# A decoder layer on one core: token turns, row statistics and roots of the last stage put in another order and on other engines

## The reference

```python
x = _layernorm(x + self_attention(x))        # 32 heads of 16, 8 key heads, causal, rotary
x = _layernorm(x + cross_attention(x, ctx))  # 32 heads of 128, 8 key heads, mask, rotary
x = _layernorm(x + clustered_ffn(x))
```

```python
def _L0_ffn_ref(input, weight, bias, centroids, assignments):
    x = input.reshape(-1, shape[-1])
    dots = jax.nn.softmax(x @ centroids.T / TEMPERATURE, axis=-1)   # 64 clusters, 0.1
    hits = dots > THRESHOLD                                          # 0.01
    query_sel = jnp.any(hits, axis=1)          # per token
    cluster_sel = jnp.any(hits, axis=0)        # per cluster, over ALL tokens
    row_sel = cluster_sel[assignments]         # per output feature
    dense = x @ weight.T + bias
    return jnp.where(query_sel[:, None] & row_sel[None, :], dense, 0)

def _layernorm(x, axis=-1, eps=1e-05):
    m, v = jnp.mean(x, ...), jnp.var(x, ...)
    return (x - m) / jnp.sqrt(v + eps)
```

## Time and profile before

| | |
|---|---|
| median of 3 runs | 811.86 us (811.58 to 813.31) |
| profiled execution, its own time | 813.68 us |
| span of the profiled execution | 811.8 us |
| PE busy | 757.1 us, 93% of the span |
| DVE busy | 600.1 us, 74% |
| POOL busy | 401.7 us, 49% |
| ACT busy | 321.0 us, 40% |
| mean granted clock of TensorE | 0.989 |

### The profile page before, as it was taken

One profiled execution on the slowest core, in us unless ns is written; L12 is line 12 of the kernel. 1 busy time (PEld: TensorE's weight loads), 2 busy tenths in 40 slices (PEclk: granted clock), 3 DMA queues, 4 the chain that ended last, 5 costly groups with the idle time before them and its releaser, 6 DMA issues.

```text
span 811.8 us, 13867 instructions
## 1 busy us (share of the span) xinstructions
PE 757.1 (93%) x4800; PEld 648.5 (80%) x4800; DVE 600.1 (74%) x1150; ACT 321.0 (40%) x680; POOL 401.7 (49%) x383
## 2 busy tenths in 40 slices
PE   4789999989999999999999999999999999999985
PEld 3677777779878887888888888888888888888763
DVE  4678888877877686677768767766776866788766
ACT  3555555563334333342333334323323423334314
POOL 7566666674544544453454445354444544354104
PEclk9899999999999999999999999999999999999998
DMA  9600004012253232322223322223322223230002
GB/s 235 149 18 17 16 16 120 3 56 53 67 142 79 53 77 58 100 53 52 78 54 77 96 57 52 52 78 76 79 78 52 52 53 98 44 93 2 1 0 103
DMA packets 107873, 53.52 MB, mean 66 GB/s; under 512 B 80448, under 2 KB 96960, under 8 KB 107840
## 3 DMA queue, kind: packets, MB, share of 16 engines
q1 hardware_dynamic: 107008, 51.51, 25.1%
q10 hardware_dynamic: 576, 1.05, 0.4%
q0 software_dynamic: 256, 0.52, 0.2%
HBM read 32.62 MB, written 2.10 MB: 43 GB/s over the span
## 4 chain that ended last, share of the span: by engine, by line
PE 67%; DVE 17%; issue 6%; POOL 4%; ACT 2%; DMA 2%; SPq 2%; DVEq 0%; POOLq 0%; ACTq 0%
PE bank L730 17%; PE bank L665 17%; PE bank L491 10%; DVE arena_r L1571 4%; PE s_bank L744 4%; PE bank L541 2%; PE s_bank L746 2%; PE bank L565 2%; PE bank L714 2%; DVE small L1659 2%; PE bank L883 2%; DVE arena_f L1653 1%; PE s_bank L714 1%; DMA arena_f<-in_L_attn_Wo 1%; PE s_bank L565 1%
## 5 line engine op out<-in xcount | busy, mean ns | idle before, releaser
L992 ACT ACTIVATE arena_r<-bank 128x256 fp32r<-128x256 f32 (+2 forms) x249 | 105.2, 459 | 219.0 <-PE bank L697 85.4
L730 PE MATMUL bank<-arena_r 128*128 128x512 f32 x768 | 191.5, 398 | 0.0
L665 PE MATMUL bank<-arena_r 128*128 128x512 f32 x720 | 185.2, 400 | 2.6 <-POOL arena_r L1430 1.6
L730 PEld LDWEIGHTS bank<-arena_r 128*128 128x128 f32 x768 | 139.6, 188 | 27.0
L665 PEld LDWEIGHTS bank<-arena_r 128*128 128x128 f32 x720 | 130.6, 188 | 32.2 <-POOL arena_r L1430 2.0
L491 PE MATMUL bank<-arena_r 128*128 128x256 f32 (+1 forms) x1056 | 146.9, 294 | 1.6 <-DVE arena_r L1571 0.8
L491 PEld LDWEIGHTS bank<-arena_r 128*128 128x128 f32 x1056 | 137.3, 191 | 9.0 <-DVE arena_r L1571 1.5
L1571 DVE TENSOR_TENSOR arena_r<-bank,arena_r 128x256 fp32r<-128x256 f32 (+2 forms) x217 | 99.8, 486 | 58.1 <-ACT arena_r L992 57.8
L992 ACT ACTIVATE arena_r<-arena_f 128x512 fp32r<-128x512 f32 (+2 forms) x178 | 104.5, 637 | 59.7 <-DMA arena_f<-arena_f 44.7
L1571 DVE TENSOR_TENSOR arena_r<-arena_f,arena_r 128x512 fp32r<-128x512 f32 (+1 forms) x95 | 89.1, 948 | 17.5 <-ACT arena_r L992 17.4
L1421 POOL TENSOR_TENSOR arena_f<-arena_f 128x512 f32<-128x512 f32 x30 | 39.1, 1305 | 116.4 <-DVE arena_f L1740 116.4
(11 more groups left out here) (164 smaller groups left out, 1180.6 us busy)
## 6 DMA issues: line engine op xcount, KB each, us to landing
arena_f<-arena_f SPq DMA_DIRECT2D x120, 128.0 KB, 2.5
...
```

The lines of the kernel that those rows point to most:

```text
L665: mm = pe.matmul(BQ2[f][:], w2q_s[a][:, e, j, f, :], xT[b][:, e, tok], start=(e == 0 and n == 0), stop=(e == EC - 1 and n == 2))
L730: mm = pe.matmul(BO2[i][:], at2[a][:, h, i * P:(i + 1) * P], w2o_s[b][:, h, :], start=(h == 0 and n == 0), stop=(h == HG - 1 and n == 2))
L992: act.activation(dst, src, ACT.Copy).then_inc(done, 1)
```

## The change

Six edits, all of them in the last fifth of the program (the loops over the slots are untouched):

1. Slot U-4 on PE: `k_turn(u + 1)` is issued right behind `pv`, ahead of the second half of the last query product; it was behind it.
2. Slots U-3 and U-2 on POOL: the first of the two `q2_low` of the next slot is issued ahead of `root` and `sum_k`; it was behind them.
3. Slot U-1 on DVE: the statistics of tile 5 are taken behind `x3_low(3)`; they were ahead of it.
4. Around the last token turns: on PE three more products of `dense(2)` come ahead of `x3_turn(6)`, so that `x3_turn(7)` follows `dots_turn(1)` at once; on ACT `x3_high(7)` comes ahead of `dots_exp(1)`; on DVE `x3_low(6)`, `dots_max(1)`, `x3_low(7)` come first, then `pick(1)` and `onehot`.
5. On PE the three products that count the hits (976) come behind a half of `dense(3)`; they were behind all of it.
6. The end: `ACT_TILES` is now 0 to 3 and is served in pairs (GpSimd's operations are 128x2); `finish` moves from DVE to POOL, behind the root; stores go out in the order 0 to 7; DVE takes `pick(t)` also for tile 4 inside the loop, ahead of `choose(t)`.

```diff
@@ constants
-        ACT_TILES = (0, 1, 2)
-        STORES = (3, 0, 4, 1, 2, 5, 6, 7)
+        ACT_PAIRS = ((0, 2), (2, 4))
+        ACT_TILES = range(4)
@@ tensor, slot(late=True)
                 pv(u, c, first)
+                if late:
+                    k_turn(u + 1, False)
...
-                if kv_next:
+                if kv_next and not late:
                     k_turn(u + 1, False)
@@ tensor, last stage
-            dense(2, first_half)
+            dense(2, range(0, 3))
             x3_turn(6)
             pe.wait_ge(f_ex, 1)
             dots_turn(1)
-            dense(2, range(2, 3))
             x3_turn(7)
...
-            dense(3, range(1, EC))
+            dense(3, range(1, 3))
...
             mm.then_inc(f_cnt, 1)
+            dense(3, range(3, EC))
@@ scalar
             x3_high(6)
+            x3_high(7)
             dots_exp(1)
-            x3_high(7)
@@ gpsimd
             normalise(U - 3)
+            q2_low(U - 2, UN - 2, 0)
             root(1, 1)
             sum_k(U - 2)
-            q2_low(U - 2, UN - 2, 0)
...
+            def mean_pair(n):
+                a, b = ACT_PAIRS[n]
+                pool.wait_ge(h_s, b)
+                pool.tensor_scalar(nmean[:, a:b], sums[:, a:b], -1.0 / E, None, ALU.mult).then_inc(h_m, 1)
+
+            def root_pair(n):
+                a, b = ACT_PAIRS[n]
+                pool.wait_ge(h_q, b)
+                pool.tensor_scalar(var8[:, a:b], ..., 1.0 / E, EPS, ALU.mult, ALU.add).then_inc(h_v, 1)
+                pool.tensor_tensor(rstd8[:, a:b], var8[:, a:b], half8[:, 0:b - a], ALU.pow).then_inc(h_v, 1)
+                pool.tensor_tensor(nmean[:, a:b], nmean[:, a:b], rstd8[:, a:b], ALU.mult).then_inc(h_v, 1)
+
+            def finish(t):
+                n = t - first
+                root(t, T + n)
+                pool.wait_ge(f_pow, T + n + 1)
+                pool.tensor_scalar(nmean[:, t:t + 1], mv8[:, 2 * t:2 * t + 1], rstd8[:, t:t + 1], -1.0,
+                                   ALU.mult, ALU.mult).then_inc(f_nm, 1)
+
+            mean_pair(0)
+            mean_pair(1)
+            root_pair(0)
+            finish(first)
+            root_pair(1)
+            for t in range(first + 1, T - 1):
+                finish(t)
+            root(T - 1, T + T - 1 - first)
@@ vector, slot U-1
-            accumulate(v - 1, c - 1, 1)
+            add_out(v - 1, c - 1, 1)
             x3_low(3)
+            dve.wait_ge(c_acc, 2 * v)
+            stats(2 * c - 1, 2 * c - 1)
...
-            dve.wait_ge(f_cr, 2)
-            dve.tensor_scalar(onehot, assign_f, cid, None, ALU.is_equal).then_inc(f_cr, 1)
-            pick(1)
             x3_low(6)
             dots_max(1)
             x3_low(7)
+            pick(1)
+            dve.wait_ge(f_cr, 2)
+            dve.tensor_scalar(onehot, assign_f, cid, None, ALU.is_equal).then_inc(f_cr, 1)
@@ vector, end
             for t in range(first, T):
+                pick(t)
                 if t > first:
-                    pick(t)
                     aggregate(t - 1, T + t - 1 - first)
                 choose(t)
-                if t > first:
-                    finish(t - 1, t - 1 - first)
                 bn_tile(t, T + t)
```

More of the change, by code:

```diff
@@ L475, in _ @@
             out_v = out.rearrange("(t p) n -> t p n", p=P)
-            for n, t in enumerate(STORES):
+            for t in range(T):
                 if t == T - 1:
@@ L1326, in scaled @@
                 if t in ACT_TILES:
-                    act.wait_ge(h_v, 3 * t + 3)
+                    act.wait_ge(h_v, 3 * (t // 2) + 3)
                 else:
@@ L1336, in _ @@
                 tile_squares(t)
-            for t in STORES:
-                if t != T - 1:
-                    scaled(t)
+            for t in range(T - 1):
+                scaled(t)
         @block.gpsimd
@@ L1550, in _ @@
             first = len(ACT_TILES)
-            for t in ACT_TILES:
-                pool.wait_ge(h_s, t + 1)
-                pool.tensor_scalar(nmean[:, t:t + 1], sums[:, t:t + 1], -1.0 / E, None, ALU.mult).then_inc(h_m, 1)
-            for t in ACT_TILES:
-                pool.wait_ge(h_q, t + 1)
-                pool.tensor_scalar(var8[:, t:t + 1], var8[:, t:t + 1], 1.0 / E, EPS, ALU.mult, ALU.add).then_inc(h_v, 1)
-                pool.wait_ge(h_v, 3 * t + 1)
-                pool.tensor_tensor(rstd8[:, t:t + 1], var8[:, t:t + 1], half8[:, 0:1], ALU.pow).then_inc(h_v, 1)
-                pool.wait_ge(h_v, 3 * t + 2)
-                pool.tensor_tensor(nmean[:, t:t + 1], nmean[:, t:t + 1], rstd8[:, t:t + 1], ALU.mult).then_inc(h_v, 1)
-                if t >= 1:
-                    root(t + 2, T + t + 2 - first)
-            for t in range(first + 2, T):
-                root(t, T + t - first)
+            def mean_pair(n):
[5 more added lines that the diff above has]
+                pool.wait_ge(h_q, b)
+                pool.tensor_scalar(var8[:, a:b], var8[:, a:b], 1.0 / E, EPS, ALU.mult, ALU.add).then_inc(h_v, 1)
+                pool.wait_ge(h_v, 3 * n + 1)
+                pool.tensor_tensor(rstd8[:, a:b], var8[:, a:b], half8[:, 0:b - a], ALU.pow).then_inc(h_v, 1)
+                pool.wait_ge(h_v, 3 * n + 2)
+                pool.tensor_tensor(nmean[:, a:b], nmean[:, a:b], rstd8[:, a:b], ALU.mult).then_inc(h_v, 1)
[13 more added lines that the diff above has]
+            root(T - 1, T + T - 1 - first)
         @block.vector
@@ L2082, in choose @@
                 dve.copy_predicated(res[:, t, :], row_i, picked[t]).then_inc(f_r, 1)
-            def finish(t, n):
-                dve.wait_ge(f_pow, T + n + 1)
-                dve.tensor_scalar(nmean[:, t:t + 1], mv8[:, 2 * t:2 * t + 1], rstd8[:, t:t + 1], -1.0,
-                                  ALU.mult, ALU.mult).then_inc(f_nm, 1)
             for t in ACT_TILES:
```

6 lines of the change are left out of this document (3 added, 3 removed).

## The result

The changed kernel takes **808.12 us** (median of 6 runs, 806.26 to 809.50); the kernel before, on the same chip in turn with it, 813.35 us (6 runs, 811.58 to 815.79). The ratio is 0.9924, with a 95% interval of 0.9903 to 0.9946: faster by 0.8%, where 1.0% was forecast (803.5 / 811.86 = 0.9897), and 4.6 us above the forecast time of 803.5, outside its range of 802.3 to 807.0. The profiled execution has a span of 803.0 us (forecast 803.4), an own time of 806.26 (forecast 805.3) and a mean granted clock of 0.994. So the trace looks as forecast and the median time doesn't; most of what follows is about that gap.

What follows compares the result with a forecast made beforehand. TensorE's work plus waits was taken as the bound up to the last dense product, VectorE's loop at the end. Terms 0.78 + 0.12 + 1.27 + 1.9 + 1.0 + 3.3 = 8.4 us off 811.86 gave 803.5 us, range 802.3 to 807.0.

Steps and rivals of the forecast that it cites:

- Parts 1 to 3: Key turn in slot U-4, first low query part, tile 5's statistics moved: 0.78 + 0.12 + 1.27 us less waiting.
- the low query part: Slots U-3 and U-2: issuing it ahead of root and key sum saves 0.12 us, with bounds 0 and 1.28.
- Last token turns: Reordering around the turns of tiles 6 and 7 starts `cluster_dots(2)` 1.9 us earlier, at 780.8 instead of 782.71.
- the new wait: TensorE, after half of `dense(3)`, would wait about 0.7 us for the count of hits, which before had cover.
- The end: VectorE rounds shrink from 2.88 to 2.48 us, tile 7 is picked when TensorE is done: 3.3 us.
- The pair power: GpSimd's power on 128x2 at the end, not in the trace, taken as 0.57 us.
- to the end of the dense products: From `cluster_dots(2)` to TensorE's last product: 19.0 - 1.7 (clock) + 0.7 (wait) = 18.0, 1.0 us less.
- Own time beyond the span: Profiled execution: span 811.8 to 803.4 us, own time 813.68 to 805.3.
- the rival: The clock falls all the same after the change, giving back 1.7 us: 805.2 us; chance 0.13.
- GpSimd as the bound: At the end, dearer pair operations or port conflicts give 1 to 4 us back: 804.5 to 807.5; chance 0.10.
- Swallowed: Little of the first three parts (2.2 us) and the turns (1.9) arrives: 807.6 us; chance 0.08.
- the slower case: New wait before the hits makes the clock fall and stay low over the dense products: 816.9 us; chance 0.05.

Runs made afterwards that it cites:

- draw: Kernel before with only the reordered last token turns and the earlier count of hits; timed ratio to the kernel before 0.9985.
- null: Kernel before, unedited, run again against itself; ratio 0.9999, medians 814.49 and 814.46 us.
- End: Kernel before with only the new end: tiles in pairs, `finish` on GpSimd, stores in order; timed ratio to the kernel before 0.9973.
- up: Kernel before with only the earlier key turn, earlier first low query part and later statistics of tile 5; timed ratio to the kernel before 0.9976.
- finish_dve: Changed kernel with `finish` back on VectorE, run twice; timed ratios to the kernel before 0.9920 and 0.9930.
- fill3: Changed kernel with `dense(4)` products ahead of the last cluster products and all of `dense(3)` ahead of the hit count; ratio to the kernel before 0.9920.
- fill3_dve: As fill3, but with `finish` on VectorE; timed ratio to the kernel before 0.9923.
- after3: Changed kernel, unedited, run once more beside fill3 on the same chip; timed ratio to the kernel before 0.9917.
- after2: Changed kernel, unedited, run again; timed ratio to the kernel before 0.9918, median 806.83 us.
- proj: Changed kernel with half an output product drawn ahead of the scores of slot U-2; timed ratio to the kernel before 0.9936.
- best: Changed kernel with the edits of both proj and fill3; timed ratio to the kernel before 0.9931.

## Why the prediction was wrong in its time and right in most of its steps

- **Parts 1 to 3, 2.17 us**: 2.24 measured. The waits went as said, and the one left before the scores of slot U-2 is VectorE's, 1.18 us. Of the 0.12 for the low query part, the row shows 0.10 (1.28 to 1.18).
- **Last token turns, 1.9, and the new wait, -0.7**: 1.2 forecast, 1.3 measured, with waits of 0.50 (0.8 forecast) and 0.40 (0.7).
- **The end, 3.3**: 3.23, by a reason that is only partly the one given. The round of 2.48 us (2.52 measured) and TensorE as the bound were right. But the prediction put the lag down to rounds of 2.88 us, and these are shorter than TensorE's 2.95 and can build up no lag; with `finish` back on VectorE they are that long again (3.05 and 2.91 us), and tile 7 is still only 0.40 us late. The lag came from the one round of 4.24 us with its wait of 1.73 for a root, and from the work of a tile that VectorE no longer does, neither of which the prediction looked at. That the number came out is in part luck. The pair power was taken 0.14 too low, which slack covers.
- **The step that failed is "to the end of the dense products"**, where 1.7 us were put down to the clock. The prediction took the fall of the earlier trace rows for an effect of the waits of the earlier trace rows and booked it as gone. The repeat has the same waits and no fall, the changed kernel's repeat has one elsewhere. The loss belonged to the execution, and the change is worth 6.8 us at equal clock instead of 8.4. That an edit makes such falls rarer stays possible: of the four traces with the wait of 1.81 us one has the fall. But draw, which cuts that wait to 0.50, has a mean span of 810.3 us over 12 executions, against 811.6 over the 18 of the kernel before on the same chip: 1.4 us less, uncertain by 1.1, where its stretch at equal clock already gives 1.3. Over all executions the mean span goes from 811.9 us (85 executions, null's among them) to 804.6 (23): 7.3 us. The spread of single executions (1.8 and 2.2 us) leaves that uncertain by about 1.0, so it cannot be told from the 6.8 of the stretch. The mean granted clock of 0.987 before and 0.990 after is no sign of fewer falls either: it counts the low clock behind TensorE's last product, where nothing waits for TensorE, and loses 3.6 and 2.6 us there in the two traces before, 1.1, 2.4 and 1.0 us in the three after. End, with all the waits, has 0.990 too, and up and draw, with the old end, have 0.987. The rivals asked only whether the clock would fall *after* the change, not whether it fell *before* by chance.
- **The level.** The forecast was laid on 811.86, the median of three runs. Executions of the kernel before lie between 810.4 and 817.8 us; the three were at the low side. They are three of the six runs whose median is 813.35, 1.5 us more, and over the 85 executions about 813.9. The range was built from costs of edits alone and had no term for this.
- **Own time beyond the span.** It was taken as unchanged (1.9). It is 2.02 us on average before and 2.45 over the 23 executions of the changed kernel, so 0.4 us are given back outside the trace.

Together: 803.5 + 2.0 (level) + 1.1 (8.4 less 7.3) + 0.4 = 807.0, which is the mean over the changed kernel's 23 executions; the 6 runs of the result lie 1.1 above. Measured as a difference of these means the change is worth 6.9 us, not 8.4. What sets the level and the own time was not tested.

**The rivals.** The clock did not fall in the first trace and did in the second, at another place: the rival was put as a question about this change, and is one about any execution. GpSimd as the bound was not seen. GpSimd's operations beside a `choose` are longer: the root takes 1.02 us instead of 0.55, and the product on 128x2 takes 0.64, ending at 795.03 with the `choose` at 795.01, where in finish_dve it takes 0.20 beside none:

```profile
794.57 0.20 POOL L1565 TENSOR_TENSOR small<-small 128x2 f32<-128x2 f32 x1
```

The Trainium skill ("SBUF — State Buffer", section "Who interferes with whom") says that VectorE and GpSimd share a port pair, which the one that issues first can hold for its whole instruction; the rows agree in this direction. In the other direction they show no cost: a `choose` takes 0.73 to 0.78 us with GpSimd beside it in the changed kernel and 0.73 to 0.77 before, and the one of fill3 that starts at 794.65, inside a power that runs from 794.13 to 794.84, takes 0.76. "Swallowed" is refuted by the sum of the parts, and the slower case by all.

**What stays open** is the own time beyond the span. It is mostly either about 2.0 or 3 us and more. In the kernels before, up and draw, with the old end, the higher value came in 2 of 109 executions; in those with the new end and `finish` on GpSimd in 24 of 55 (7 of these 164 lie between 2.3 and 2.9 and are counted as low). Both finish_dve runs (1 of 12) spoke for GpSimd's product as the cause; fill3_dve, without it, had it in 4 of 9, and that theory fell. Repeats differ much: after3 has 0 of 6, fill3 6 of 6. From VectorE's last scaling to the end of the span it takes 803.0 - 800.54 = 2.46 us, as before, so nothing in the trace shows it. It comes with the new end, and the cause is open.

## What to carry over

Before a loss of clock is booked as something that an edit removes, run the unedited kernel a second time: if the same waits stand there without the fall, the loss belongs to the execution and only the waits may be counted. Before a lag is put down to the length of a round, compare the round with that of the engine it runs behind, and look for the one round that is longer. Give a forecast as a difference, and widen its range by the spread of the reference runs, which here (7 us) was as large as the whole gain. Fill a wait with work that covers nothing itself: in this kernel dense products were such work, half an output product was not.

## What the runs showed of the chip beyond expectation

- The clock's fall from 2.4 to 1.2 GHz in the stretch: none in null, up, draw, end, both finish_dve, fill3_dve and two of the three traces of the changed kernel, but at 784 (before), 733 (after2, fill3), 745 (proj) and 746 us (best), 1.7 or 3.4 us lost each time, inside or up to 1.6 us behind a wait of TensorE of 1.2 to 1.8 us. The waits of 1.18 and 1.81 us are passed at full clock in other executions.
- At the start of the program every trace loses at least 3.4 us of clock (seven windows from 19 us on in the changed kernel). It is 5.1 us in end, 6.8 in fill3 and 8.5 in up and after3, by a longer or a second stretch at 1.2 GHz, so this too differs between executions.
- A power on 128x2 takes 0.71 us on GpSimd, on 128x1 0.55; its TENSOR_SCALAR on 128x2 (L1561) takes 0.19 and its product on 128x2 0.20, where no `choose` stands beside them.
- The time outside the recorded span differs by over 1 us between executions of one program, and between two ends of the program.
